# Three edits in a grouped matrix product with Winograd's form of Strassen's scheme: residual loads on GpSimd's queue, the bias in the pair's own step, sums of weights laid out by partition

## The reference, cut to what matters

```
y    = einsum('bsi,boi->bso', x, weight[adapter_ids])
h    = einsum('bsd,nrd->nbsr', y, lora_A)
low  = einsum('nbsr,nor->bso', h, lora_B * (2 * lora_weights)[:, None, None])
out  = x + (einsum('bsd,od->bso', y, W) + bias + low)
```

## Time and profile before

| | us |
|---|---|
| median of three runs (1510.13 to 1513.56) | 1511.92 |
| time of the profiled execution | 1515.89 |
| its span, first to last instruction | 1514.1 |
| PE busy in the span | 1422.2 (94%) |
| DVE busy | 1178.9 (78%) |
| ACT busy | 475.7 (31%) |
| GpSimd (POOL) busy | 364.5 (24%), none of it after 740 us |

### The profile page before, as it was taken

The page is one execution under the profiler, slowest core; times in us unless marked ns, Lnnn a source line. Parts: engine busy times, 40 slices in busy tenths (PEclk is TensorE's granted clock), DMA queues, the critical chain, the costliest instruction groups (busy, mean ns, idle before and its releaser), DMA issues.

```text
span 1514.1 us, 32881 instructions
## 1 busy us (share of the span) xinstructions
PE 1422.2 (94%) x5882; PEld 1100.6 (73%) x5883; DVE 1178.9 (78%) x1772; ACT 475.7 (31%) x681; POOL 364.5 (24%) x683
## 2 busy tenths in 40 slices
PE   7999899999999999999956899999999999999997
PEld 4887778888887887877845686777777677767765
DVE  8866777687878686688816789888888888888887
ACT  5343444444544344344412122112211221122121
POOL 4365445555443645656000000000000000000000
PEclk9999999999999999999988899999999999999999
DMA  8968567677775676688577455656555655555554
GB/s 267 303 197 242 161 205 218 210 236 226 216 216 185 195 227 224 194 248 260 185 195 229 114 149 141 152 131 155 136 150 141 151 140 149 140 148 144 135 143 111
DMA packets 177327, 279.01 MB, mean 184 GB/s; under 512 B 33280, under 2 KB 145408, under 8 KB 169088
## 3 DMA queue, kind: packets, MB, share of 16 engines
q1 hardware_dynamic: 124576, 137.96, 35.0%
q10 hardware_dynamic: 27680, 82.33, 17.6%
q0 software_dynamic: 25024, 58.24, 12.6%
HBM read 194.51 MB, written 83.89 MB: 184 GB/s over the span
## 4 chain that ended last, share of the span: by engine, by line
SPq 35%; issue 21%; PE 19%; DVE 12%; DMA 3%; ACT 3%; DVEq 2%; ACTq 2%; POOL 1%; POOLq 1%
SPq L330 22%; SPq L271 8%; PE ps L1085 6%; PE ps L1089 6%; PE ps L1092 6%; DVE w_lo L788 4%; SPq L340 3%; DVE rows_by L723 2%; DVE x_turn L819 2%; ACT w_hi L504 2%; DMA w_place<-in_L_cond_weight_dram 1%; DVEq L271 1%; POOL x_raws L283 1%; DMA bias_sb<-in_L_ffn_bias_dram 1%; SPq L283 1%
## 5 line engine op out<-in xcount | busy, mean ns | idle before, releaser
L283 POOL DMA_DIRECT2D x_raws<-in_x_dram x560 | 299.7, 535 | 333.3 <-issue 163.1
L1198 PE MATMUL ps<-w_hi,op_hi 128*128 x896 | 258.8, 411 | 48.4 <-ACT op_hi L639 26.6
L1203 PE MATMUL ps<-w_hi,op_lo 128*128 x896 | 250.1, 401 | 12.5 <-DVE op_lo L952 12.5
L1085 PE MATMUL ps<-w_hi,x_both 128*128 (+1 forms) x976 | 249.7, 397 | 11.6 <-issue 5.7
L1200 PE MATMUL ps<-w_lo,op_hi 128*128 x896 | 248.9, 400 | 0.0
L1198 PEld LDWEIGHTS ps<-w_hi,op_hi 128*128 128x128 f32 x896 | 162.9, 189 | 118.1 <-issue 87.1
L1089 PE MATMUL ps<-w_hi,x_both 128*128 (+1 forms) x976 | 248.2, 396 | 0.0
L1092 PE MATMUL ps<-w_lo,x_both 128*128 (+1 forms) x976 | 247.4, 395 | 0.0
L1085 PEld LDWEIGHTS ps<-w_hi,x_both 128*128 128x128 f32 x976 | 183.5, 188 | 59.5 <-issue 13.2
L1089 PEld LDWEIGHTS ps<-w_hi,x_both 128*128 128x128 f32 x976 | 183.6, 188 | 45.1
L1092 PEld LDWEIGHTS ps<-w_lo,x_both 128*128 128x128 f32 x976 | 182.9, 187 | 44.9
(11 more groups left out here) (123 smaller groups left out, 863.5 us busy)
## 6 DMA issues: line engine op xcount, KB each, us to landing
w_place<-in_L_cond_weight_dram SPq DMA_DIRECT2D x480, 128.0 KB, 4.2
y_scr<-rows_by ACTq DMA_DIRECT2D x72, 512.0 KB, 5.0
x_raws<-in_x_dram POOLq DMA_DIRECT2D x560, 64.0 KB, 3.4
x_raws<-y_scr SPq DMA_DIRECT2D x512, 64.0 KB, 2.5
rows_by<-in_x_dram SPq DMA_DIRECT2D x128, 256.0 KB, 4.6
out_dram<-rows_by ACTq DMA_DIRECT2D x128, 256.0 KB, 4.1
weff<-fold_sb POOLq DMA_DIRECT2D x8, 512.0 KB, 11.2
piece_raw<-weff POOLq DMA_DIRECT2D x64, 64.0 KB, 4.1
```

Of the source, the lines that this page charges most:

```text
L283: eng.dma_start(x_raw[b][BLK * q:BLK * (q + 1), 2 * h:2 * h + 2, :], rows[:, :, q * SEG:(q + 1) * SEG]).then_inc(loaded, 16)
L1085: mm(ps[b][:, cols], x_hi[b][:, t, :], hi[t], start=t == 0, stop=False)
L1198: mm(bank[i], op_hi[q][i][:, t, :], hi[t], start=t == 0, stop=False)
L1203: last = mm(bank[i], op_lo[q][i][:, t, :], hi[t], start=False, stop=t == KH - 1)
```

## The change

It has three parts. (1) `load_rest` moves from SP's queue to the end of GpSimd's, where it follows the last `store_piece`. (2) The bias is added to pair p's rows in `out_step(p, q)`, after the transposes and sums of pair p+1 and before the first take of pair p, and not in the step before; DVE's wait for the bias moves behind the transposes and rests of pair 0. (3) The sums of weights are kept as four DRAM tensors in which the partition is the slowest dimension; a piece is stored by four DMAs and not two; T2 is loaded by two DMAs and not eight, and of the two 3 MB loads the `_lo` one is issued from SP's queue.

```
-        comb_hi = nc.dram_tensor("comb_hi", [PIECES, P, HALF], f32, kind="Internal").ap()
-        comb_lo = nc.dram_tensor("comb_lo", [PIECES, P, HALF], f32, kind="Internal").ap()
+        comb_hi = nc.dram_tensor("comb_hi", [P, PIECES, P], f32, kind="Internal").ap()
+        combs_hi = nc.dram_tensor("combs_hi", [P, PIECES, 3 * P], f32, kind="Internal").ap()
...
@@ SP, load_y @@
-                elif u % 2 == 0:
-                    sp.wait_ge(y_turned, group * 8 + (4 * (u // 2) - 4))
+                elif u == 0:
+                    sp.wait_ge(y_turned, group * 8 - 4)
                 for p in range(2):
                     sp.wait_ge(stored[p], stores[p])
+                if u == 2 and not (isinstance(group, int) and group == 0):
+                    sp.wait_ge(y_turned, group * 8)
...
@@ SP, main line @@
-            load_rest(0, 0, w_ready, sp.snap(ranks * CHUNKS + CHUNKS))
             for u in range(2, RING):
                 load_y(u, 0, u)
-            for b in range(2):
-                sp.wait_ge(stored[b], 16 * (SLOTS // 2))
-            load_rest(1, 1)
+            other = sp.snap((entry(sp, n_ranks, 0, EXPERTS) + 1) % 2)
+            sp.wait_ge(piece_free, PIECES + 1)
+            sp.wait_ge(tile_done, SLOTS)
+            sp.dma_start(beside(w_lo, other).rearrange("p g f -> p (g f)").bitcast(f32),
+                         combs_lo.rearrange("p g f -> p (g f)")).then_inc(other_combs, 16)
...
-            load_pair(1, 0)
-            with sp.Fori(0, PAIRS // 2 - 2) as g:
-                load_pair(g + 1, 1)
-                load_rest(g * 2 + 2, 0, out_stored[0], sp.snap(g * 64 + 64))
-                load_pair(g + 2, 0)
-                load_rest(g * 2 + 3, 1, out_stored[1], sp.snap(g * 64 + 64))
-            load_pair(PAIRS // 2 - 1, 1)
             for q in range(2):
-                load_rest(PAIRS - 2 + q, q, out_stored[q], 64 * PAIRS // 2 - 64)
+                load_pair(1, q)
+            with sp.Fori(2, PAIRS // 2) as g:
+                for q in range(2):
+                    load_pair(g, q)
...
@@ GpSimd, store_piece @@
-                for comb, held in ((comb_hi, piece_hi), (comb_lo, piece_lo)):
-                    pool.dma_start(comb[bass.ds(i, 1)].rearrange("a p f -> (a p) f"),
-                                   held[:, :, :].rearrange("p b m -> p (b m)").bitcast(f32)).then_inc(piece_stored, 16)
+                for comb, combs, held in ((comb_hi, combs_hi, piece_hi), (comb_lo, combs_lo, piece_lo)):
+                    pool.dma_start(comb[:, bass.ds(i, 1), :].rearrange("p a f -> p (a f)"),
+                                   held[:, T2, :].bitcast(f32)).then_inc(piece_stored, 16)
+                    pool.dma_start(combs[:, bass.ds(i, 1), :].rearrange("p a f -> p (a f)"),
+                                   held[:, T1:, :].rearrange("p b m -> p (b m)").bitcast(f32)).then_inc(piece_stored, 16)
...
@@ GpSimd, behind the last piece; load_rest itself is as it was on SP @@
+            ranks = entry(pool, n_ranks, 0, EXPERTS)
+            load_rest(0, 0, w_ready, pool.snap(ranks * CHUNKS + CHUNKS))
+            for b in range(2):
+                pool.wait_ge(stored[b], 16 * (SLOTS // 2))
+            load_rest(1, 1)
+            with pool.Fori(0, PAIRS // 2 - 1) as g:
+                for q in range(2):
+                    load_rest(g * 2 + (q + 2), q, out_stored[q], g * 64 + 64)
...
@@ ACT @@
                 for comb, held in ((comb_hi, w_hi), (comb_lo, w_lo)):
-                    for c in range(CHUNKS // 2):
-                        act.dma_start(held[:, bass.ds(par, 1), CHUNKS // 2 + c, 0:KH, :].rearrange("p a t m -> p (a t) m").bitcast(f32),
-                                      comb[c * 4:(c + 1) * 4, :, T2 * P:(T2 + 1) * P].rearrange("g p f -> p g f")).then_inc(first_comb, 16)
+                    act.dma_start(held[:, bass.ds(par, 1), CHUNKS // 2:CHUNKS, 0:KH, :].rearrange("p a c t m -> p (a c) (t m)").bitcast(f32),
+                                  comb[:, :, :].rearrange("p (c g) f -> p c (g f)", g=4)).then_inc(first_comb, 16)
...
-            for comb, held in ((comb_hi, w_hi), (comb_lo, w_lo)):
-                act.dma_start(beside(held, other).bitcast(f32), comb[:, :, P:HALF].rearrange("g p f -> p g f")).then_inc(other_combs, 16)
+            act.dma_start(beside(w_hi, other).rearrange("p g f -> p (g f)").bitcast(f32),
+                          combs_hi.rearrange("p g f -> p (g f)")).then_inc(other_combs, 16)
...
@@ DVE, out_step, behind turn_pair(p + 1, 1 - q) @@
+                dve.wait_ge(rest_loaded[q], rests)
+                add_bias(q)
                 dve.wait_ge(rest_biased, p * 2 + 2)
                 take(p, q, A12, 0, 0)
...
-                if not last:
-                    dve.wait_ge(rest_loaded[1 - q], rests)
-                    add_bias(1 - q)
                 take_common(p, q, S3, 1)
...
@@ DVE, ahead of the first step @@
-            dve.wait_ge(bias_loaded, 16)
-            dve.wait_ge(rest_loaded[0], 64)
-            add_bias(0)
             wait_y(0, 16 * 2 * QUADS)
             turn_pair(0, 0)
             for i in range(OPS):
                 split_op(0, 0, i)
+            dve.wait_ge(bias_loaded, 16)
             out_step(0, 0, 16 * 2 * QUADS, 64)
```

More of the change, by code:

```diff
@@ L70, in grouped_adaln_ffn_kernel @@
         y_scr = nc.dram_tensor("y_scr", [POS, TOK, D], f32, kind="Internal").ap()
-        comb_hi = nc.dram_tensor("comb_hi", [PIECES, P, HALF], f32, kind="Internal").ap()
-        comb_lo = nc.dram_tensor("comb_lo", [PIECES, P, HALF], f32, kind="Internal").ap()
+        comb_hi = nc.dram_tensor("comb_hi", [P, PIECES, P], f32, kind="Internal").ap()
+        combs_hi = nc.dram_tensor("combs_hi", [P, PIECES, 3 * P], f32, kind="Internal").ap()
+        comb_lo = nc.dram_tensor("comb_lo", [P, PIECES, P], f32, kind="Internal").ap()
+        combs_lo = nc.dram_tensor("combs_lo", [P, PIECES, 3 * P], f32, kind="Internal").ap()
         EXPERT_BYTES = KT * D * 4
@@ L331, in load_y @@
                                      rows[:, :, q * SEG:(q + 1) * SEG]).then_inc(y_loaded[b], 16)
[L333 to L341, removed]
             def load_next_expert(slot):
@@ L382, in _ @@
                 load_next_expert(SLOTS - AHEAD + u)
-            ranks = entry(sp, n_ranks, 0, EXPERTS)
-            load_rest(0, 0, w_ready, sp.snap(ranks * CHUNKS + CHUNKS))
             for u in range(2, RING):
                 load_y(u, 0, u)
-            for b in range(2):
-                sp.wait_ge(stored[b], 16 * (SLOTS // 2))
-            load_rest(1, 1)
+            other = sp.snap((entry(sp, n_ranks, 0, EXPERTS) + 1) % 2)
[3 more added lines that the diff above has]
+                         combs_lo.rearrange("p g f -> p (g f)")).then_inc(other_combs, 16)
             def load_pair(g, q):
@@ L484, in _, with load_rest @@
                 load_x(RING * g + 3, 3)
-                pool.wait_ge(piece_stored, g * 32 - 64)
+                pool.wait_ge(piece_stored, g * 64 - 128)
                 pool.nop().then_inc(piece_free, 1)
             store_piece(PIECES - 1)
-            pool.wait_ge(piece_stored, 32 * PIECES)
+            pool.wait_ge(piece_stored, 64 * PIECES)
             pool.nop().then_inc(piece_free, 1)
+            def load_rest(p, q, free=None, count=0):
+                samples = [entry(pool, order_sample, 4 * p + s, SAMPLES - 1) for s in range(4)]
+                if free is not None:
+                    pool.wait_ge(free, count)
+                for s in range(4):
+                    pool.dma_start(out_rows[q][s * BLK:(s + 1) * BLK, :, :],
+                                 x[bass.ds(samples[s], 1)].rearrange("a (j m) n -> (a j) m n", m=2)).then_inc(rest_loaded[q], 16)
+            ranks = entry(pool, n_ranks, 0, EXPERTS)
[6 more added lines that the diff above has]
+                    load_rest(g * 2 + (q + 2), q, out_stored[q], g * 64 + 64)
         @program.scalar
@@ L1022, in _ @@
                 split_op(0, 0, i)
+            dve.wait_ge(bias_loaded, 16)
             out_step(0, 0, 16 * 2 * QUADS, 64)
             with dve.Fori(0, PAIRS // 2 - 1) as g:
-                out_step(g * 2 + 1, 1, g * 128 + 256, g * 64 + 128)
+                out_step(g * 2 + 1, 1, g * 128 + 256, g * 64 + 64)
                 out_step(g * 2 + 2, 0, g * 128 + 256, g * 64 + 128)
-            out_step(PAIRS - 1, 1, 0, 0, True)
+            out_step(PAIRS - 1, 1, 0, 32 * PAIRS, True)
             route_steps[:] = [spread_step, compared_step, opened_step, slots_step, listed_step]
@@ L1188, in pair_products @@
                         if i == S2:
-                            pe.wait_ge(first_comb, 16 * CHUNKS)
+                            pe.wait_ge(first_comb, 32)
                         elif i == S1:
```

## The result

| | before | after |
|---|---|---|
| time, median (lowest to highest) | 1512.74 us (1510.13 to 1513.65), 4 runs | 1445.86 us (1443.62 to 1448.63), 4 runs |
| ratio after/before, 95% interval | | 0.9561, 0.954 to 0.9583 |
| profiled execution, its span | 1515.89, 1514.1 | 1448.63, 1446.8 |
| granted TensorE clock, mean | 0.984 | 0.984 |

The change makes the kernel 4.4% faster. That is the forecast's direction, 14 us above its 1432 and inside its range. The same kernel run again in a later set gave 1447.12 us (0.9579, 0.9551 to 0.9606).

The account below looks back on a forecast made before the run. SP's issuing was taken to bound the pair steps, PE next. Terms - 52 - 30 + 1 + 3 - 2 = - 80 us on 1515.9 give 1436, or 1432 us as median; range 1416 to 1460.

Parts of the forecast that it names:

- SP's issuing bounds the pair: Pair steps: SP's issuing alone fills each pair's 21.58 us; relieved, a pair takes 19.85 us, 52 us less over 30 pairs.
- the residual's 10 us of spare time: Pair steps: with its loop spanning two steps, the residual lands 10 us before the bias needs it.
- GpSimd beside DVE: Pair steps: DVE won't hold up GpSimd's descriptor writing; residual issues stay near 0.53 us each.
- PE straight on into pair 0: End of stage one: PE starts pair 0 at 779.3 us without waiting for the bias, 18 us earlier.
- Between the stages: From stage one's end to pair 2: earlier bias, `y` and 3 MB loads start pair 2 at 827, not 857: 30 us less.
- land at about 789: Between the stages: pair 1's `y`, issued some 5 us earlier, lands then and DVE turns it; PE loses 6 us.
- just in time: Before S1 of pair 0: the 3 MB loads take 24 us and land at 809, S1 starting at 809.5.
- The first rival: Before S1: the 3 MB loads come no sooner, S1 starts at 818.7, 9 us later, kernel 1441 us; chance 0.09.
- Stage one: Stage one: two more stores per piece lengthen DVE's waits for GpSimd; + 3 us, ends 0 and 14.
- The tail: End of kernel: DVE, no longer behind PE, has one take left; 2 us less.
- the + 1 of DVE's late start: Start of pair 2: DVE begins some 10 us late and gains 1 us per pair; costs 1 us.
- The range's upper end: Whole kernel: 1458 from 20.2 us per pair (+ 11), late loads (+ 9), stage one at half its end (+ 6), rounded to 1460.

Follow-up runs that it names:

- the word early: GpSimd's word that a piece's buffer is free given between the fourth tile's load halves: changed kernel so edited 1434.54 us, kernel before so edited 1502.85 us.

## Why the prediction was right, and where it was wrong

**SP's issuing bounds the pair: right.** Moving four issues off SP, with the bias where it was, takes the pair from 21.58 to 20.09 us. The pair came out at 19.73 where 19.85 was taken and PE's own 19.74 was one end, 55.4 us less and not 52. SP's 16.8 us per pair came out at 17.0, the residual's 10 us of spare time at about 10, its issues at 0.49 us where 0.53 was taken. Each mark of being right that was named for this step is in the rows: no wait of DVE for the residual, waits of SP for `y_turned`, PE at 19.7. The bias step gives only the last 0.36 us per pair, and only when SP is relieved.

**GpSimd beside DVE: right.** 128 issues of L491 last 489 ns at the least and in the middle and 510 at the most, beside a DVE that is busy for 95% of the pair steps (562.25 of 591.9 us). The trap that the Trainium skill describes in "SBUF — State Buffer" shows in no row; the trace bears out that the operations of this kernel don't spring it.

**PE straight on into pair 0: right.** It works from 785.5 to 797 without a pause; DVE's 33 us at the bias are gone.

**Between the stages: right in kind, wrong in size.** 15.8 us and not 30. The failed term is that pair 1's `y` would "land at about 789". From the end of stage one it was to be 9.8 us (789 - 779.2), and it was 23.8 (809.25 - 785.5): 14.0 us, all that is missing. Of these, 2.3 us are that the issues ended 7.3 us after the end of stage one and not 5.0 (789.2 less some 5, less 779.2). The other 11.7 are the landing, taken as 4.8 us (789 - 784.2) and measured at 16.5. From the landing on, the prediction's steps hold: 20.5 us to S1 forecast, 21.3 measured; then 17.5 and 17.0 to pair 2. One of its marks of being wrong, DVE waiting for `y`, stands in the rows, for 19.53 us. The prediction took a landing from a time when nothing of 3 MB was in flight, and asked of the 3 MB loads only when they would land themselves: "just in time" at 809. For that it took 24 us, and the later one took 24.1; it landed at 817.8 and was not waited for, since S1 was later still. It counted the longer rows as a gain only. They are the cost: with rows of 1.5 KB the `y` lands in 6.4 us, and the later 3 MB load, at 815.5, is still 3.3 us ahead of S1.

**The first rival, 3 MB loads no sooner: wrong in its reason.** Loads as slow as 27 us each (old layout) cost 0.75 us; that kernel is faster than the change. What the Trainium skill, "DMA: Bandwidth & Descriptors", section "Issuing engines are not separate DMA queues", leaves for part 3, a layout that is worth all and a queue that is worth nothing, doesn't hold in its first half: with parts 1 and 2 in place the layout costs 13 us. Whether the second queue by itself brings anything was not tried.

**Stage one: right in sign, in its range, too small.** + 6.3 us and not + 3 (range 0 to 14). The further growth of DVE's wait is 9.7 us, and PE did not have enough ahead of it. In the kernels with four stores per piece, whose word stands behind both halves, stage one ends at 782.4 to 785.8 (mean 784.7 of six), in those with two at 779.1 to 783.2 (780.7 of four). The ranges overlap a little, and the means differ by 4 us; with the word early it is 769.2 us with two stores and 770.7 to 772.7 with four, 1.5 to 3.5 us. So 2 to 4 us of the 6.3 are the stores', and the rest is within what stage one varies by.

**The tail: right,** - 2.4 us for - 2.

**The sum:** - 55.4 - 15.8 + 6.3 - 2.4 against - 51 - 30 + 3 - 2 (the + 1 of DVE's late start counted with the pairs). The pair steps gave 4 us more, stage one took 3 more, and pair 1's late `y` took 14. So the forecast is in its range with one term off by half, and 4 us of that were offset by luck. The range's upper end has a slip: stage one at half its end, 7 us, is 4 us above the 3 of the sum and not 6, which makes 1456; the result is inside either way.

## What to carry to other kernels

Count what a queue issues in one turn of the loop, the register reads between the issues too: here 20 issues and their reads filled 21.6 us, and nothing but the late data showed it. When a bulk load is started just ahead of small loads that work waits for, look at its row length: here long rows made the first of two such loads faster and the small loads late, and shorter rows, or asking for the small ones first, was better as long as the bulk load wasn't the one awaited. A word that a buffer is free belongs in an in-order queue ahead of long work that it doesn't depend on.

## What was not expected of the hardware

- Two 3 MB loads in 128 rows of 24 KB each: the first went faster than in rows of 1.5 KB (15.1 us against 24.1), the second did not (24.1 against 23.9), and a 64 KB load in short rows issued between them took 16.5 us to land in place of 6.4.
- Pauses of PE cost more than they last: behind a pause of 3.66 us eight matmuls took 3.78 us in place of 2.03, and at the restart between the stages four took 2.07 in place of 1.11, with a granted clock of 0.50 from 811 to 818.9 us, the lower of its two levels.
- The same part changed its sign with what stood beside it: layout and second queue took 4.8 us off the kernel before, and the layout put 13 us on to the other two parts.
